# Second attention on the context: scores at the end of odd slots, minima of four heads at once, and bank-freeing steps ahead of minima and exponentials

## What is computed

```python
def _L1_xattn_ref(x, cond, mask, wq, bq, wk, bk, wv, bv, wo, bo):
    # B = 8 batches, N = L = 256 rows, C = 512, H = 16 heads of D = 32
    q = _w8a8_linear(x, wq, bq).reshape(B, N, H, D).transpose(0, 2, 1, 3)
    k = (cond @ wk.T + bk).reshape(B, L, H, D).transpose(0, 2, 1, 3)
    v = (cond @ wv.T + bv).reshape(B, L, H, D).transpose(0, 2, 1, 3)
    scores = jnp.einsum('bhnd,bhld->bhnl', q, k) * inv_sqrt_d + mask[:, None]
    attn = jax.nn.softmax(scores, axis=-1)
    o = jnp.einsum('bhnl,bhld->bhnd', attn, v)
    o = o.transpose(0, 2, 1, 3).reshape(B, N, C)
    return _w8a8_linear(o, wo, bo)
```

## Time and profile before

| what | value |
|---|---|
| median of 3 runs | 2317.35 us (2317.33 to 2318.66) |
| profiled execution, its own time | 2319.68 us |
| its span | 2317.8 us |
| PE busy | 2098.1 us (91%), 13663 instructions |
| DVE busy | 1305.4 us (56%) |
| ACT busy | 1031.1 us (44%) |
| POOL busy | 892.2 us (38%) |
| mean granted clock of TensorE | 0.960 of full |
| scores of the second attention on the context, first and last start | 1914.32 and 2223.82 us |

### The profile page before, as it was taken

One profiled execution on the slowest core, in us unless ns is written; L12 is line 12 of the kernel. 1 busy time (PEld: TensorE's weight loads), 2 busy tenths in 40 slices (PEclk: granted clock), 3 DMA queues, 4 the chain that ended last, 5 costly groups with the idle time before them and its releaser, 6 DMA issues.

```text
span 2317.8 us, 37875 instructions
## 1 busy us (share of the span) xinstructions
PE 2098.1 (91%) x13663; PEld 1668.6 (72%) x13677; DVE 1305.4 (56%) x3359; ACT 1031.1 (44%) x2318; POOL 892.2 (38%) x944
## 2 busy tenths in 40 slices
PE   7799999899999987999999999988999868888877
PEld 6688888687777875887777788866565446676645
DVE  3454445654555455644537633356777756667767
ACT  3332333444434433445542222324666546677753
POOL 1753444334343322214433024634444335445302
PEclk9899999899999998999999999998999988999988
DMA  3402101111111111111101011123333410000001
GB/s 129 137 33 69 46 33 51 46 42 46 49 46 43 41 39 53 44 35 53 47 27 39 27 37 37 66 35 56 52 57 51 108 57 15 15 29 7 15 1 73
DMA packets 58312, 109.05 MB, mean 47 GB/s; under 512 B 7184, under 2 KB 35088, under 8 KB 54672
## 3 DMA queue, kind: packets, MB, share of 16 engines
q1 hardware_dynamic: 58128, 106.63, 15.8%
HBM read 86.10 MB, written 4.26 MB: 39 GB/s over the span
## 4 chain that ended last, share of the span: by engine, by line
PE 42%; DVE 11%; ACT 6%; issue 3%; POOL 1%; SPq 0%; DMA 0%; ACTq 0%; DVEq 0%; POOLq 0%
PE PS L1330 18%; ACT xP L2628 3%; PE PS L1838 3%; PE PS L1938 3%; PE PS L1346 2%; DVE st L200 2%; DVE aM L2086 2%; PE PS L1906 1%; DVE PS L2746 1%; PE PS L2487 1%; PE PS L993 1%; PE PS L1005 1%; PE PS L1926 1%; PE PS L2524 1%; PE PS L1893 1%
## 5 line engine op out<-in xcount | busy, mean ns | idle before, releaser
L1330 PE MATMUL PS<-WH,bXH 128*128 128x512 f32 x640 | 258.2, 403 | 0.0
L1330 PE MATMUL PS<-WL,bXH 128*128 128x512 f32 x640 | 250.2, 391 | 0.0
L1330 PE MATMUL PS<-WH,bXL 128*128 128x512 f32 x640 | 250.1, 391 | 0.0
L1511 DVE SCALAR_TENSOR_TENSOR s<-s,PS 128x256 f32<-128x256 f32 x160 | 67.3, 421 | 294.7 <-ACT s L1462 294.5
L2086 DVE TENSOR_REDUCE aM<-PS 128x4 f32<-128x1024 f32 x128 | 153.7, 1221 | 49.3 <-PE PS L1906 48.4
L1462 ACT ACTIVATE s<-PS 128x256 f32<-128x256 f32 x160 | 61.6, 386 | 261.9 <-PE PS L1330 261.2
L1632 POOL TENSOR_TENSOR WL<-sg,WH 128x512 fp32r<-128x512 f32 x80 | 102.0, 1310 | 184.3 <-ACT WH L1446 184.3
L421 PE MATMUL PS<-aXH,QKH 128*128 128x512 f32 x384 | 157.3, 410 | 16.0 <-ACT sq L634 7.9
L1627 POOL TENSOR_TENSOR mixed<-mixed,s 128x256 f32<-128x256 f32 x112 | 82.6, 741 | 225.5 <-DVE s L1528 225.4
L421 PE MATMUL PS<-aXH,QKL 128*128 128x512 f32 x384 | 152.6, 397 | 0.0
L421 PE MATMUL PS<-aXL,QKH 128*128 128x512 f32 x384 | 152.6, 397 | 0.0
(11 more groups left out here) (403 smaller groups left out, 6054.2 us busy)
## 6 DMA issues: line engine op xcount, KB each, us to landing
sg<-in_gu SPq DMA_DIRECT2D x16, 1024.0 KB, 4.9
gQK<-in_Wqk SPq DMA_DIRECT2D x16, 768.0 KB, 6.2
gC<-in_Wc SPq DMA_DIRECT2D x16, 512.0 KB, 6.4
lgB<-gate_sums SPq DMA_DIRECT2D x32, 256.0 KB, 4.5
aqs<-aQH SPq DMA_DIRECT2D x64, 128.0 KB, 4.2
xN<-in_xT SPq DMA_DIRECT2D x4, 1024.0 KB, 10.8
xN<-in_x SPq DMA_DIRECT2D x4, 1024.0 KB, 7.6
cst<-in_cT SPq DMA_DIRECT2D x8, 512.0 KB, 3.7
```

The lines of the kernel that those rows point to most:

```text
L1330: mm = e.matmul(PS[:, b, :], x[:, kc, c:c + 128], y[:, kc, :], start=kc == 0 and n == 0, stop=kc == KC - 1 and n == 2)
```

## The change

Only orders within slots change, and one step is split in two; no arithmetic, no tile and no buffer. `scores` go from order 2.5 to 9.5, the last place in their slot (odd ones), but for the first of all. VectorE's part of `soft` gets a name of its own, `minima`, and a place of its own: the odd pair's goes to the even slot before, so that the minima of four heads follow on each other. `soft` is now ScalarE's exponentials alone, at 1.2. `flip` of an odd pair, which stands in an even slot, goes to 0.8, ahead of the exponentials; that of an even pair stays at 2. `key_high` and `key_low` from batch 1 on go to 0.4 and 0.6, `scale_out` to 0.5, `project_out` and `value_out` to 0.7, all ahead of minima and exponentials; for batch 0 they stay where they were.

```diff
--- before.py
+++ after.py
@@ -2309,23 +2309,24 @@
         put(base - 12 - first, 5, "turn", j)
         put(base - 12 - first, 9, "turned", j)
         put(base - 11 - first, 5, "scale", j)
-        put(base - 10 - first, 3 if j != 1 else 1.6, "scale_out", j)
+        put(base - 10 - first, 3 if j == 0 else 0.5, "scale_out", j)
         for i in range(4):
             put(base - 9 + i - (5, 0, 0)[min(j, 2)], 5, "key", j, i)
-            put(base - 8 + i - (5, 0, 0)[min(j, 2)], 1.5, "key_high", j, i)
-            put(base - 8 + i - (5, 0, 0)[min(j, 2)], 4, "key_low", j, i)
+            put(base - 8 + i - (5, 0, 0)[min(j, 2)], 0.4 if j else 1.5, "key_high", j, i)
+            put(base - 8 + i - (5, 0, 0)[min(j, 2)], 0.6 if j else 4, "key_low", j, i)
         for i in (0, 1):
             put(base - 8 + 2 * i if j else i - 10, 5, "project", j, i)
-            put(base - 7 + 2 * i if j else i - 9, 2 if j == 0 else 1.7 if j == 1 else 3, "project_out", j, i)
+            put(base - 7 + 2 * i if j else i - 9, 2 if j == 0 else 0.7, "project_out", j, i)
             put(base - 6 + 2 * i if j else i - 8, 3 if j else 2.2, "project_low", j, i)
             put(base - 4 + 2 * i if j else i - 8, 5 if j else (5.5, 2)[i], "value", j, i)
-            put(base - 3 + 2 * i if j else -7, 3 if j else 9, "value_out", j, i)
+            put(base - 3 + 2 * i if j else -7, 0.7 if j else 9, "value_out", j, i)
         put(base - 4 if j else -16, 6, "mask", j)
         for i in range(8):
             if U == 2 or i % 2 == 0:
-                put(base + i - 1 if j or i else -7, 2.5, "scores", j, i // (U // 2))
-            put(base + i, 1, "soft", j, i)
-            put(base + i + 1, 2, "flip", j, i)
+                put(base + i - 1 if j or i else -7, 9.5 if j or i else 2.5, "scores", j, i // (U // 2))
+            put(base + i - i % 2, 1, "minima", j, i)
+            put(base + i, 1.2, "soft", j, i)
+            put(base + i + 1, 0.8 if i % 2 else 2, "flip", j, i)
         for g in range(4):
             put(base + 2 * g + 3, 5, "pv", j, g)
             put(base + 2 * g + 3, 9, "pv_out", j, g)
@@ -2732,7 +2733,7 @@
                         last = e.scalar_tensor_tensor(out=QF[:, m, :], in0=PS[:, b, 256 * (m % 2):256 * (m % 2) + 256],
                                                       scalar=swI[:, m:m + 1], in1=sxB[:, :], op0=ALU.mult, op1=ALU.mult)
                     last.then_inc(p_dq.sem, 1)
-                elif what == "soft":
+                elif what == "minima":
                     n = 8 * j + i
                     if i == 0:
                         e.wait_ge(*mk_neg.upto(j + 1))
```

## The result

The changed kernel takes 2327.75 us (median of 5, 2325.65 to 2330.11), the kernel before beside it 2317.51 (2317.33 to 2320.44): a ratio of 1.0042, 95% interval 1.0027 to 1.0056. It is slower by 0.4%; the forecast was 2313, range 2302 to 2323. The profiled execution of the changed kernel took 2325.65, span 2323.9, against 2319.68 and 2317.8 before.

The account below looks back on a forecast made before the run. TensorE was taken to bound the kernel, busy 136.04 of 155.46 us in batches 2 to 5. Terms +3.5 + 0.4 - 3.2 - 2.2 - 2.3 = -3.8 from the median 2317.35 gave 2313.55, rounded to 2313; range 2302 to 2323.

Parts of the forecast that it names:

- late4's hand-over: Batch 1, round 2 to 3: small VectorE step of the former stage's norm; the prediction named no wait for it.
- the middle: Batches 2 to 5, 155.46 us before: forecast 159.0, so 3.5 slower.
- the round's chain: From one four-head group's scores to the next: turnings, copies and exponentials in sequence; plain batch 39.15 us against 38.18.
- the stall before even turnings: Each round: TensorE ready at 4.1 or 4.55, even pair only at 5.0; new stall of 0.9 or 0.45 us.
- Round 3 to 0: From a batch's last group's scores to the next batch's first: key behind the even pair's copy, 9.3 us.
- Lead-in: Batches 0 and 1: second scores 3.5 us later, later rounds faster; net 0.4 slower, uncertain by 4.
- minima no longer stand behind newton steps: Lead-in's last three rounds: minima also freed from weights_out and fin's quotients; these rounds 2.85 us faster.
- Batch 6: Batch 6, 38.61 us before: rounds of 9.85, 9.15, 8.8 and 7.6, together 35.4, so 3.2 faster.
- Batch 7: Batch 7's first three rounds, 28.49 us before: 25.25, less fast by 1.0 for the lower clock, so 2.2 faster.
- Last stretch: From the last scores to the last turning, 10.59 us before: 2.3 faster.
- rival 2: Every round: late hand-overs at each odd slot's third single-bank user and queued VectorE releases cost 0.4 more; 2322 us; chance 0.22.
- Rival 3: Drain: clock stays at its lower level, two more pieces at up to 1 us each; 2315 us; chance 0.05.

Follow-up runs that it names:

- e12_fill_tr: Changed kernel plus 16 idle transposes ahead of the wait for each even pair of batch 7; its first three rounds took 7.89, 8.74, 8.84 us.
- e15_lead_fill: Changed kernel plus 28 idle transposes ahead of scale's wait in batch 1; 2322.39 us in one time.
- e2_late: Changed kernel with late4, the last step of the former stage's norm, moved from slot 12 to the end of slot 13; 2325.53 us in one time.
- e7_half_copy: Changed kernel with the copy of each turned pair moving only half its columns from the fifth pair on; 2314.55 us in one time.
- e3_copy_first: Changed kernel with the even pair's copy moved ahead of the odd pair's exponentials (order 1.1 for 2); 2339.21 us in one time.
- e11_fill_mm: Changed kernel plus 12 idle matmuls ahead of the wait for each even pair of batch 7; its first three rounds took 7.89, 8.72, 8.84 us.

## Why the prediction was wrong

**The step that failed** is the price of the new gaps. The prediction took them at their length and carried the granted clock of before over into the rounds behind them: 1.0 us in the drain and nothing in the lead-in. Measured, the clock's lower level cost 3.9 in batch 7 (e12_fill_tr) and 3.6 in the first two rounds (e15_lead_fill), and 1.5 more in two later rounds of the profiled execution. A second step failed on its own: late4's hand-over behind eight minima, put at nothing, is 1.8 (e2_late). Of the stage's miss of 11.9, 7.9 is the clock's (beyond the 1.0 priced) and 1.8 late4's; the remaining 2.2 is spread over the middle (1.4) and the other stretches. Term by term:

- **What bounds the kernel, and the round's chain**: right. The chain of the earlier trace rows came out to a tenth at every step, the stall before even turnings was 0.76 for 0.9 said, and a plain batch took 39.3 for 39.15. e7_half_copy and e3_copy_first show which links bind: VectorE's key_low in round 0 to 1, the copy in 1 to 2 and 2 to 3.
- **Round 3 to 0**: 9.57 for 9.3. I counted it by the copy; it is bound by TensorE's own work behind a stalled turning, with 1.1 from the turning's start to the next for the 0.79 that I had counted. Over the four such rounds of the middle that is 0.9 (0.5 in the plain ones, 0.3 in those with statistics). Another 0.85 lies in batch 4, where rounds 1 to 2 and 2 to 3 took 9.62 and 11.23: before fin TensorE waits 1.09 there for key_low's release on VectorE, where key_low stands behind eight minima and the norm's newton steps. All other rounds together gave 0.3 back.
- **Lead-in**: the term that failed most, +0.4 said with 4 of doubt, +7.8 measured. The new first gap was priced as a gap (3.5 later) and not for what the clock makes of the work behind it: 3.6 over the first two rounds (e15_lead_fill). A further 0.6 in the sixth and 0.9 in the seventh are the clock's as well, and came and went between kernels that are the same there. The other part, 1.8, is late4's hand-over (e2_late). The step "minima no longer stand behind newton steps" looked at what minima wait for, and not at what waits for minima.
- **Batch 6**: 3.2 faster said, 2.8 measured.
- **Batch 7**: 2.2 faster said, 0.8 slower measured. The rounds' chain was right (e12_fill_tr); the clock was priced at 1.0 over three rounds and cost 3.9. The price came from the earlier trace rows, which I misread: the line shows four of fin's transposes only because the view ended there. The group has eight and took 1.97, and 1.91 in the changed kernel, for 1.04 at full clock. The change makes one gap of 3.08 before each even turning. Before, there were two, of 1.8 ahead of the turning and 1.6 ahead of the scores:

```profile
2201.14 1.06 PE L2537 MATMUL PS<-idF,xP 128*128 128x128 f32 x8 [1.83 <-ACT xP L2628]
2203.79 0.58 PE L2524 MATMUL PS<-xKH,xQH 32*128 32x256 f32 x4 [1.58 <-ACT xP L2628]
```

  What ran slow behind the latter, scores and out, had the exponentials' wait still to come, so that much of it was hidden.
- **Last stretch**: 2.3 faster said, 2.6 measured.
- **Rivals**: the kernel is on the slower side, at 2327.75 above rival 2's 2322, but not by its mechanism in every round, since hand-overs at the third single cost no tenth more than said. The other half of that rival, releases on VectorE that queue behind eight minima, did show, in single rounds: batch 4 (0.85), and late4 in batch 1. Rival 3 (the clock stays at its lower level in the drain) is what happened, at 3.9 where 1.0 and the rival's 2 more were said, and it had a counterpart in the lead-in that no rival covered. The rule that I cited beside it, the Trainium skill, "TensorE: Matmul & The Clock Gate", Part 4, that transposes don't count as TensorE being busy as matmuls do, isn't what made it so: in e12_fill_tr idle transposes held the clock just as idle matmuls did in e11_fill_mm.
- **The range**: it took in bounds for banks and hand-overs, and none for the clock, though the earlier trace rows showed two levels in the very stretches where I made gaps longer. A bound was in the rows: all the work of a round at half speed.

## What to carry to other kernels

A new gap on TensorE costs its own length and, where the granted clock falls behind it, it can cost as much again in the work that follows (the first gap grew by 3.0, and the first two rounds lost 3.6 more to the clock); when an order moves waits together into one longer gap, price that work at both levels. For each group of steps that is moved ahead on an in-order engine, list what is then behind it, the small steps of other stages too, and who waits for them. Before you call a difference of a microsecond or two in one trace an effect of the order, look at the granted clock of that round, and at other kernels with the same order there. A better order can lose in seams and lead-in what it wins elsewhere: here it paid in the last batch alone, where TensorE has little else to do (0.9974 with the idle time filled).
